# Attention, slots and experts on one core: the identity ahead of R's load, LayerNorm 3 in three units, and shorter last batches in both phases

## The reference

```python
# phase 1: linear attention with 16 heads of 8 features, on LayerNorm 1
h = layernorm(x)
q, k, v = split_heads(h @ Wq.T + bq), ...            # k and v likewise
f = lambda t: exp(t/sqrt(8) @ R - 0.5*sum((t/sqrt(8))**2, -1))
kv = einsum('bhnd,bhne->bhde', f(k), v)
x = x + einsum('bhnd,bhde,bhn->bhne', f(q), kv, 1/sum(f(q), -1)) @ Wo.T + bo

# slots: 16 slots a batch attend to the rows (LayerNorm 2), one slot an expert
xn = layernorm(x)
o = slot_query + mha(slot_query, xn, xn, d_W..., d_b...)
hs = layernorm(o) * ln_g + ln_b                      # "LayerNorm 3"
y = (silu(hs @ W1 + b1) * silu(hs @ Wg + bg)) @ W2 + b2   # its own W for each of 16 experts
o = o + y

# phase 2: the rows attend to the 16 slots
out = x + mha(xn, o, o, c_W..., c_b...)
```

## Time and profile before

| | |
|---|---|
| median of 3 runs | 189.96 us (189.78 to 190.16) |
| profiled execution | 189.91 us, of which the span of instructions is 187.9 |
| busy in the span | PE 176.2 us (94%), POOL 140.2, DVE 134.7, ACT 118.7 |
| chain that ended last, by engine | PE 81%, ACT 5%, POOL 5%, issue 5%, DVE 4% |
| granted clock | 1.00 |

### The profile page before, as it was taken

One profiled execution on the slowest core, in us unless ns is written; L12 is line 12 of the kernel. 1 busy time (PEld: TensorE's weight loads), 2 busy tenths in 40 slices (PEclk: granted clock), 3 DMA queues, 4 the chain that ended last, 5 costly groups with the idle time before them and its releaser, 6 DMA issues.

```text
span 187.9 us, 4852 instructions
## 1 busy us (share of the span) xinstructions
PE 176.2 (94%) x1538; PEld 134.7 (72%) x1538; DVE 134.7 (72%) x386; ACT 118.7 (63%) x295; POOL 140.2 (75%) x276
## 2 busy tenths in 40 slices
PE   3979999999999999999999999989989999999992
PEld 3845677768877787778877867823755789888992
DVE  2448897877786987667769577656538999979840
ACT  2036466787779868667777767239405876856871
POOL 6195889978898996894979496306948968787983
PEclk9999999999999999999999999999999999999999
DMA  3819994999999400000000000000000001102113
GB/s 93 265 25 313 382 280 127 378 325 372 297 375 235 141 20 5 2 5 0 0 3 0 3 2 0 5 0 0 3 3 0 0 31 58 56 28 68 50 58 112
DMA packets 20828, 19.36 MB, mean 103 GB/s; under 512 B 1434, under 2 KB 16227, under 8 KB 20803
## 3 DMA queue, kind: packets, MB, share of 16 engines
q1 hardware_dynamic: 20066, 18.46, 31.3%
q10 hardware_dynamic: 704, 0.59, 1.0%
q0 software_dynamic: 32, 0.00, 0.2%
HBM read 16.95 MB, written 2.10 MB: 101 GB/s over the span
## 4 chain that ended last, share of the span: by engine, by line
PE 81%; ACT 5%; POOL 5%; issue 5%; DVE 4%; POOLq 0%; DVEq 0%
PE ps L1169 15%; PE ps L1244 7%; PE ps L1417 6%; PE ps L1463 6%; PE ps L1179 4%; PE ps L1282 4%; PE ps L1225 4%; PE ps L1202 4%; PE ps L1451 3%; PE ps L1099 3%; PE ps L1192 2%; PE ps L1440 2%; PE ps L1236 2%; PE ps L1215 2%; PE ps L1356 2%
## 5 line engine op out<-in xcount | busy, mean ns | idle before, releaser
L1169 PE MATMUL ps<-Wproj,xnT 128*128 128x512 f32 x64 | 30.5, 600 | 1.4 <-ACT xnT L621 1.4
L522 POOL TENSOR_TENSOR Wgs<-Wgs,W2s 128x256 f32<-128x256 f32 x31 | 18.7, 627 | 1.5 <-DVE W2s L1065 1.5
L886 DVE TENSOR_REDUCE ss<-sq 128x64 f32<-128x512 f32 x16 | 10.9, 683 | 10.0 <-ACT sq L597 10.0
L1169 PEld LDWEIGHTS ps<-Wproj,xnT 128*128 128x128 f32 x64 | 11.0, 190 | 9.7 <-issue 7.6
L1463 PE MATMUL ps<-W1s,W2s 128*128 128x128 f32 x128 | 17.3, 279 | 0.7 <-ACT W2s L725 0.7
L590 ACT ACTIVATE pr<-ps,nmax 128x256 f32<-128x256 f32 x32 | 14.8, 469 | 4.3 <-DVE nmax L925 3.9
L1463 PEld LDWEIGHTS ps<-W1s,W2s 128*128 128x128 f32 x128 | 15.8, 191 | 2.2 <-ACT W2s L725 1.8
L1244 PE MATMUL ps<-XN2T,Ad 128*128 128x256 f32 x64 | 16.6, 382 | 0.0
L531 POOL TENSOR_TENSOR W2s<-W2s,X 128x256 f32<-128x256 f32 x15 | 10.8, 727 | 6.3 <-ACT W2s L731 3.3
L450 POOL TENSOR_SCALAR xn<-X,nm,rs 128x127 f32<-128x127 f32 x30 | 14.0, 476 | 1.6
L424 POOL TENSOR_TENSOR qz<-ft,rz 128x256 f32<-128x256 f32 x16 | 10.1, 630 | 5.8 <-DVE rz L875 5.3
(11 more groups left out here) (194 smaller groups left out, 495.8 us busy)
## 6 DMA issues: line engine op xcount, KB each, us to landing
W1s<-in_L_ffn_e_W_dram SPq DMA_DIRECT2D x4, 1024.0 KB, 7.8
Wgs<-in_L_ffn_e_Wg_dram SPq DMA_DIRECT2D x4, 1024.0 KB, 8.3
W2s<-in_L_ffn_e_W_dram SPq DMA_DIRECT2D x16, 256.0 KB, 8.2
out_dram<-W2s SPq DMA_DIRECT2D x16, 128.0 KB, 1.7
X<-in_L_attn_x_dram SPq DMA_DIRECT2D x3, 512.0 KB, 7.1
hbias<-in_L_ffn_e_bg_dram SPq DMA_DIRECT2D x8, 64.0 KB, 2.0
X<-in_L_attn_x_dram ACTq DMA_DIRECT2D x2, 128.0 KB, 3.7
X<-in_L_attn_x_dram ACTq DMA_DIRECT2D x1, 256.0 KB, 5.0
```

What stands on the lines that cost most here:

```text
L522: last = pool.tensor_tensor(heads(at[:, k, j * HS:(j + 1) * HS], S), heads(ep[:, k, j * HS:(j + 1) * HS], S), over(rsm[:, k, j * H:(j + 1) ...
L886: ve.tensor_reduce(ss[:, k, :].rearrange("p (j h) -> p j h", j=2), sq[:, k].rearrange("p j (h d) -> p j h d", d=DH), AX.X, ALU.add).then_i ...
L1169: last = pe.matmul(banks(b)[:, j, :], xnT[:, k, j * P:(j + 1) * P], Wproj[:, :], start=True, stop=True)
```

## The change

The identity is built ahead of the issue of R's load, and there are 7 warm-up products in place of 14. LayerNorm 3 goes in units of 1, 1 and 2 groups. The last group's slots lie in bank 4, so the experts' first products have four banks in turn in place of five, and the way out goes in units of 2, 1 and 1 groups. At the end of phase 1 the last batch's slots are read straight from PSUM, its sums lie in bank 5, and fewer products with the identity are issued. In phase 2 the last batch is taken in halves from the maxima to the store, and its two halves are stored apart. The written orders of all engines in both phases are new.

```diff
-BANK_UP = tuple((2, 4, 5, 6, 3)[i % 5] for i in range(2 * G))
+BANK_UP = tuple((2, 5, 6, 3)[i % 4] for i in range(2 * G))
+UNITS = ((0, 1), (1, 2), (2, 4))
+PLACE = ((0, 0), (0, P), (1, 0), (4, 2 * P))
+OUT_UNITS = ((0, 2), (2, 3), (3, 4))
+BANK_OUT = (2, 2, 7)
+BANK_K, BANK_V = 6, 5
+K15 = (NB - 1) % RING
+BANK_TT, BANK_OP = (5, 0), (7, 1)
+        def slots_at(g):
+            return ps[:, PLACE[g][0], PLACE[g][1]:PLACE[g][1] + P]
...
 # SP: the last batch's store
+            for j in range(2):
+                sp.wait_ge(ob_dve, j + 1)
+                half = slice(j * P, (j + 1) * P)
+                sp.dma_start(out_rows[:, NB - 1, half], ob[:, K15, half]).then_inc(stored[K15], 16)
...
 # POOL
-            load(pool, r_in, (Rrep[:, :], R.unsqueeze(0).broadcast_to([H, DH, DH])))
             own(pool.memset(ident[:, :], 0.0))
             pool.affine_select(out=ident[:, :], in_=ident[:, :], compare_op=ALU.not_equal, fill=1.0, base=0,
                                pattern=[[-1, P]], channel_multiplier=1).then_inc(ident_ok, 1)
+            load(pool, r_in, (Rrep[:, :], R.unsqueeze(0).broadcast_to([H, DH, DH])))
...
-            apply2(11); apply1(15); add_bias(13); experts_masks(); scale_features(13); rstd2(12); apply2(12)
...
+            rstd2(13); apply2(13); scale_features(15); rstd2(14); apply2(14); rstd2(15); experts_masks()
             wait(pool, mbp_ok, NB)
             pool.memset(hT[:, :, :], 0.0).then_inc(hT_zero, 1)
             out_bias(0, 8)
-            for half in range(2):
+            for n, (first, end) in enumerate(UNITS):
...
-            pack_keys(1); scale2(0); pack_values(0)
+            pack_keys(1); pack_values(0); pack_values(1); scale2(0)
...
-            scale2(12); scale2(13); scale2(14); add_kept(10); add_kept(11); scale2(15); add_kept(12); add_kept(13)
-            add_kept(14)
+            scale2(12); add_kept(9); add_kept(10); scale2(13); scale2(14); add_kept(11); add_kept(12); scale_half(0)
+            add_kept(13); add_kept(14)
...
 # ACT
             def set_bias(n):
                 i = 5 + n
-                sc.wait_ge(sg_ok, i - 4)
+                sc.wait_ge(sg_ok, i - 3)
...
+            def exp_half(j):
+                half = slice(j * HS, (j + 1) * HS)
+                sc.wait_ge(sx_ok, NB + j)
+                sc.activation(ep[:, K15, half], sx[:, K15, half], ACT.Exp).then_inc(ep_ok, 1)
+            def keep_at_half(j):
+                sc.wait_ge(tt_ok, NB + j)
+                sc.activation(atT[:, K15, :, j * P:(j + 1) * P], ps[:, BANK_TT[j], 0:2 * P]..., ACT.Copy).then_inc(atT_ok, 1)
...
 # DVE
+            def last_residual():
+                ve.wait_ge(pr_ok, NB)
+                ve.tensor_tensor(slots_at(3), slotr[:, 3, :], d_bo_all[:, :], ALU.add).then_inc(slots_set, 1)
...
+                outputs = ps[:, 7, 0:EG * S].unsqueeze(1) if end == NB else pvr[:, first:end, :]   # in slot_heads
...
-            slot_stats(0); slot_stats(1); slot_apply(0); slot_apply(1); slot_gains(0); slot_gains(1)
+            slot_stats(0); slot_moments(0); slot_stats(1); slot_moments(1); slot_apply(0); slot_stats(2)
+            slot_gains(0); slot_apply(1); slot_moments(2); slot_gains(1); slot_apply(2); slot_gains(2)
...
-            maxima2(15); shift2(15); sums2(15); norms2(15); scale_last(); add_rows(15)
+            maxima_half(0); shift_half(0); sums_half(0); norms_half(0); maxima_half(1); shift_half(1); sums_half(1)
+            norms_half(1); scale_half(1); add_rows_half(0); add_rows_half(1)
...
 # PE
-            warm(9); turn_biases(); turn_weights(); warm(3); feature_weights(); warm(2); turn_xn(0); project(0)
+            warm(5); turn_biases(); warm(1); turn_weights(); feature_weights(); turn_xn(0); warm(1); project(0)
...
-            turn_xn2(15); fill(); turn_pr(14); scores(15); slots(14); queries(0); fill(); slot_values(15)
-            queries(1); turn_pr(15); slot_sums(3); fill(); queries(2); slots(15); queries(3); fill(); slot_sums(4)
-            fill()
+            slot_values(13); turn_pr(13); scores(14); slots(13); slot_values(14); slot_sums(2); turn_xn2(15)
+            turn_pr(14); scores(15); slots(14); queries(0); fill(); queries(1); slot_sums(3); turn_pr(15)
+            slot_values(15); queries(2); slot_sums(4); slots(15); fill(); queries(3); fill()
...
-            for _ in range(8):
+            for _ in range(1):
                 pe.matmul(ps[:, BANK_TURN, 0:P], ident[:, :], ident[:, :], start=True, stop=True)
...
-            experts_in(0, 0); turn_xh(1); experts_in(0, 1); experts_in(1, 0); experts_in(1, 1); experts_in(2, 0)
+            experts_in(0, 0); turn_xh(1); experts_in(0, 1); experts_in(1, 0); turn_xh(2); experts_in(1, 1)
+            hidden_bias(2, 0); experts_in(2, 0)
...
-            experts_out(2); turn_slots(0); experts_out(3); slot_keys_values(0); turn_slots(1)
-            slot_keys_values(1)
+            experts_out(2); turn_slots(0); experts_out(3); turn_slots(1); slot_keys_values(0)
+            turn_slots(2); slot_keys_values(1); slot_keys_values(2)
...
-            value_weights(3); turn_at(9); scores2(14); outputs2(9); turn_at(10); scores2(15); turn_at(11)
-            outputs2(10); turn_at(12); outputs2(11); turn_at(13); outputs2(12); turn_at(14); outputs2(13)
-            outputs2(14); turn_at(15); outputs2(15)
+            turn_at(10); scores2(14); outputs2(9); outputs2(10); turn_at(11); turn_at(12); scores2(15); outputs2(11)
+            turn_at(13); outputs2(12); turn_at(14); outputs2(13); outputs2(14); turn_at_half(0); turn_at_half(1)
+            outputs_half(0); outputs_half(1)
```

More of the change, by code:

```diff
@@ L75 @@
 VSET = NB // 4
-BY_DVE = (15,)
-def done(b, on_dve):
-    return sum((n in BY_DVE) == on_dve for n in range(b + 1))
+K15 = (NB - 1) % RING
+BANK_TT, BANK_OP = (5, 0), (7, 1)
 def build(nc, x, a_Wq, a_bq, a_Wk, a_bk, a_Wv, a_bv, a_Wo, a_bo, R, slot, d_Wq, d_Wk, d_Wv, d_Wo,
@@ L974, in slot_stats @@
-            def slot_stats(half):
-                ve.wait_ge(o_ok, half + 1)
-                for g in (2 * half, 2 * half + 1):
-                    last = ve.bn_stats(st3[:, g, :], ps[:, half, (g % 2) * P:(g % 2 + 1) * P])
+            slot_heads(3); slot_outputs(3); last_residual(); slot_weights_of_sums(4); slot_heads(4); slot_outputs(4)
+            def slot_stats(n):
+                ve.wait_ge(o_ok, UNITS[n][1] // 3 + 1)
+                for g in range(*UNITS[n]):
+                    last = ve.bn_stats(st3[:, g, :], slots_at(g))
@@ L1378, in experts_out, with turn_slots @@
                 last.then_inc(y_ok, 1)
-            def turn_slots(half):
-                pe.wait_ge(o2s_ok, half + 1)
-                for g in range(2):
-                    last = pe.transpose(ps[:, 2, (2 * half + g) * P:(2 * half + g + 1) * P], o2[:, 2 * half + g, :],
+            def turn_slots(n):
+                first, end = OUT_UNITS[n]
+                pe.wait_ge(o2s_ok, n + 1)
+                if n == 1:
+                    pe.wait_ge(o2_ok, 1)
+                for g in range(first, end):
+                    last = pe.transpose(ps[:, BANK_OUT[n], (g - first) * P:(g - first + 1) * P], o2[:, g, :],
```

423 lines of the change are left out of this document (237 added, 186 removed).

## The result

The changed kernel takes 188.35 us (median of 7 runs, 187.42 to 190.19) beside 189.78 of the kernel before on the same chip: ratio 0.9938 (95% interval 0.9912 to 0.9963), about 1.2 us. The forecast was 186.9; the time lies at the number of the rival in which half rate holds through project(0) (188.2). The profiled execution took 188.97 us with a span of 187.2, against 187.9 before.

The account below looks back on a forecast made before the run. TensorE, busy 65.65 of 65.65 us in the long stretch, was taken as the bound, leaving gains only at the seams: 0.8 + 0.3 + 0.5 + 0.4 + 1.0 = 3.0; 189.91 - 3.0 = 186.9 us, range 183.6 to 189.6.

Parts of the forecast that it names:

- the rival in which half rate holds through project(0): Start: TensorE stays at half rate, so the start loses 0.5 us instead of gaining 0.8; 188.2 us, chance 0.15.
- The start: Kernel start, up to project(0): earlier identity and fewer warm-ups gain 0.8 us, between 2.1 gained and 0.5 lost.
- Middle: Phase 1's middle: nothing from TensorE's busy stretch, 0.3 us from the ramp between projections 0 and 4.
- Slower: Long stretch of phase 1: a long step queued ahead of one TensorE waits for; 190.4 us at 0.32 a batch, chance 0.10.
- No change: Whole kernel: half rate at the start and 0.2 us lost a batch give 189.9 us; chance 0.07.
- End of phase 1 and LayerNorm 3: Last slots through LayerNorm 3 to the first experts: of 0.9 + 1.4 us earned, 0.5 arrives.
- late by 0.6: LayerNorm 3: with the masks moved, GpSimd is some 0.6 us late for the earlier statistics.
- the 0.9 of the end of phase 1: End of phase 1: direct PSUM read, slot_sums(4) put earlier and two fewer fills bring slot statistics 0.9 us earlier.
- last_residual, put at nothing: End of phase 1: adds some 0.3 us on VectorE where it stands idle for 0.84, so costs nothing.
- Way out: Slots' way out after the last expert: one group instead of two, four shorter links save 0.4 us (0.2 to 0.7).
- End of phase 2: Last batches of phase 2: batch 15 in halves shortens the last links, gaining 1.0 us (0.1 to 1.6).
- One issue more on a queue that waits anyway: End of phase 2: the extra store of the last batch was given no cost.

Follow-up runs that it names:

- e9_after: The changed kernel itself, unaltered, measured a second time: 187.96 us beside 189.46 of the kernel before, ratio 0.9934.
- the bridge: Changed kernel with five more warm-up products at the start, three ahead of feature_weights and two behind it: 188.28 us, 0.9938 of the kernel before.
- R first: Changed kernel with R's load issued ahead of the identity again, its reduced warm-ups kept: 187.62 us, 0.9912 of the kernel before.
- e3_masks: Changed kernel with experts_masks moved back to the middle of phase 1 in GpSimd's list, behind add_bias(12): 193.72 us, 1.0086 of the kernel before.
- e7_silu: Changed kernel with silu(0, 0) and silu(0, 1) ahead of slot_gains(2) in VectorE's list: 188.26 us, 0.9924 of the kernel before.
- e11_masks_away: Changed kernel with two selects of experts_masks at the start and one ahead of rstd2(15): 189.17 us, 0.9983 of the kernel before.
- e16_way_out: Changed kernel with keep_slots2(2) ahead of keep_o2T(1) in VectorE's list: 188.22 us, 0.9891 of the kernel before.

## Why the prediction failed, point by point

**The start: the step that failed.** The prediction put the start at a gain of 0.8, as a middle between full and half rate. It had R landing at 6.7 to 7.1 (it was used at 6.22, in `e9_after` at 6.82), project(0) at 8.5 to 8.9 (8.79) and the two rates. The middle is what failed. With a pause of 0.89 to 1.93 us ahead of feature_weights, project(0) began at half rate in all twelve profiles with the changed start and took 2.97 to 3.77 us by the chain (in five of them the rate rose within it); in all six with the bridge or R first it took 1.95 to 2.02. The gain to project(1) was 0.0, in `e9_after` a loss of 0.56. Argued against the rival was that TensorE works closely from 2.1 to 5; but its ten passes there take 2.50 us, 0.25 each, where the four at 9.20 before took 0.15 or less, so it was still at half rate when the pause came. The Trainium skill, "TensorE: Matmul & The Clock Gate", section "The HAM clock gate", had the rule, half rate by default until sustained activity lifts it, and again after idleness; the passes from 1.60 to 12.54 agree with the first part, while the second is not seen at the start, where the rate had not risen yet. The bridge shows that the pause kept the rate low.

That the time came out at this rival's 188.2 is partly luck: it took 0.5 off at the start, where nothing was lost, and kept 2.2 us for the other steps, of which 1.3 came to the last add. In the profile 0.7 of the forecast 3.0 us reached the end of the span; 0.8 is missing from the start, 0.2 from the middle, 0.4 from the way out and 0.9 from the end, 0.6 of that by the stores.

**Middle.** 0.1 for 0.3; project(1) to project(15) took 80.80 us beside 80.88. The *Slower* rival did not come, but `e3_masks` shows a case of its mechanism: TensorE stood 2.41 us for apply2 behind the masks. The sum of *No change* is not consistent: half rate (188.2) and 0.2 a batch over 11 batches make 190.4; 189.9 has a start that neither gains nor loses.

**End of phase 1 and LayerNorm 3: the sum met, two steps of it wrong.** The first silu was foreseen at 125.2 (125.14) and set_bias(0) at 126.55 (126.45), and `e7_silu` shows slot_gains(2) as the reason. But GpSimd was not late by 0.6: without the masks ahead of it the root came no earlier. Nor did the 0.9 of the end of phase 1 come from its terms: in `e11_masks_away`, where VectorE's slot steps are as long as before (0.96, 0.68, 0.88 and the last rsel 0.19), o comes 23.69 us after project(15), before it came 23.78. What the moved masks did instead is shift the start of out_bias against VectorE's steps: project(15) to set_bias(0) takes 32.15 us with the short steps and 33.22 with the long ones, against 32.62 before. So the edit gives 0.5 or costs 0.6, and both profiles of the changed kernel hold the gain; the prediction had nothing that decides between them, so that the sum was met is luck. And last_residual, put at nothing, took 0.70 beside out_bias, with rsel behind it at 0.53 in place of 0.19: 0.2 on the path. Reading slots from PSUM saved its 0.25 (the product starts 0.06 after the last pass), but slot_outputs(4) then starts 0.46 behind VectorE's sum, in every profile, where the prediction took the 0.28 of before away; I found no reason for it.

**Way out.** 0.0 for 0.4. The prediction summed four shorter links and did not look at VectorE's order: the last copy came behind keep_o2T(1), 3.48 us after turn_act in place of 3.11. `e16_way_out` brings back 0.3.

**End of phase 2.** The links were right in kind and 0.7 in place of 1.0 in size, shown by two kernels. "One issue more on a queue that waits anyway" was wrong: the second store waits behind the issue of the first, which took 0.33 and 1.39 us in the two profiles of this code, and lost 0.6 in the one with 1.39.

## What to carry to other kernels

Before moving a load behind something, ask which of the two the last arrival is: here the identity came early for nothing and R late for everything, and the pause also kept TensorE's clock low. A price between "full rate" and "half rate" should not be averaged; look at the spacing of the passes ahead and for the idle stretch behind them. In an in-order list, a shorter step gains nothing until one has read what stands ahead of it there, and work placed in "idle time" should be priced beside what the neighbouring engine does then.
